# A recommendation tower on one core: the last layer with its input as the stationary operand and the weight as one moving column

## What is computed

```python
e = jnp.stack([tbl_f[ids[:, f]] for f in range(27)], axis=1)     # 2048 x 27 x 128
dot = jnp.einsum('bnd,bmd->bnm', e, e)                           # all pairs of features
z = flat[:, idx]                                                 # the 351 pairs i < j
h = jnp.concatenate([z, dense_ctx], axis=1)                      # 2048 x 367
h = jnp.maximum(h @ W_top1 + b_top1, 0.0)                        # 512
h = jnp.maximum(h @ W_top2 + b_top2, 0.0)                        # 256
y = h @ W_top3                                                   # 2048 x 1
```

## Time and profile before

| | |
|---|---|
| median of 3 runs | 385.35 us (384.9 to 387.28) |
| the profiled execution's time | 387.6 us |
| its span, first to last instruction | 385.8 us |
| TensorE busy | 345.6 us, 90% of the span |
| GpSimd busy | 251.8 us, 65% |
| VectorE busy | 251.6 us, 65% |
| ScalarE busy | 124.3 us, 32% |
| granted TensorE clock, mean | 0.969 of full speed |

### The profile page before, as it was taken

How to read it: one execution, slowest core, us unless ns; L and a number is a source line. 1 busy time by engine, 2 the same in 40 slices (tenths; PEclk the granted TensorE clock), 3 DMA queues, 4 the chain that set the end, 5 groups by cost and what they waited for, 6 DMA issues and landing times.

```text
span 385.8 us, 14180 instructions
## 1 busy us (share of the span) xinstructions
PE 345.6 (90%) x6216; PEld 308.1 (80%) x6216; DVE 251.6 (65%) x757; ACT 124.3 (32%) x235; POOL 251.8 (65%) x271
## 2 busy tenths in 40 slices
PE   0875899889799999999999999999999999997686
PEld 0764788778699888998899878997899978995675
DVE  4898597767576677666876658675876668742031
ACT  2554234232133332333233223333233322335122
POOL 5777777777777777777777777775777667730000
PEclk9999699899699999999999999999999999999699
DMA  7998843357634763446534754547433744344420
GB/s 187 262 259 206 209 103 93 77 138 157 101 82 93 166 137 87 95 110 169 114 83 98 166 126 99 88 99 175 110 78 91 162 115 100 63 85 99 76 49 1
DMA packets 59215, 46.39 MB, mean 120 GB/s; under 512 B 38499, under 2 KB 53186, under 8 KB 59153
## 3 DMA queue, kind: packets, MB, share of 16 engines
q1 hardware_dynamic: 50705, 28.16, 32.8%
q0 software_dynamic: 8448, 17.32, 19.8%
HBM read 38.37 MB, written 7.09 MB: 118 GB/s over the span
## 4 chain that ended last, share of the span: by engine, by line
PE 68%; POOL 18%; issue 8%; DVE 3%; DMA 2%; ACT 1%; POOLq 0%
PE onehot_ps L592 20%; POOL rows L352 18%; PE onehot_ps L594 14%; PE dots_ps L620 10%; PE tile_ps L604 6%; PE mlp_ps L626 5%; PE mlp_ps L628 5%; PE mlp_ps L627 5%; PE mlp_ps L661 2%; DVE mask L493 2%; DMA rows<-tbl,idx 2%; DMA idx<-ids_gather 1%; DVE z_lo L531 1%; DVE h_lo L538 0%; ACT h_hi L401 0%
## 5 line engine op out<-in xcount | busy, mean ns | idle before, releaser
L352 POOL DMA_INDIRECT rows<-tbl,idx x264 | 251.0, 951 | 89.7 <-issue 76.6
L493 DVE TENSOR_SCALAR mask<-idb,cmp 125x256 fp32r<-125x256 int32 x672 | 210.4, 382 | 78.2 <-PE onehot_ps L594 72.9
L592 PE MATMUL onehot_ps<-mask,tab_hi 125*128 125x256 f32 x672 | 187.0, 312 | 19.5 <-DVE tab_lo L500 9.5
L594 PE MATMUL onehot_ps<-mask,tab_lo 125*128 125x256 f32 x672 | 171.3, 285 | 0.0
L592 PEld LDWEIGHTS onehot_ps<-mask,tab_hi 125*128 125x128 f32 x672 | 130.1, 194 | 34.7 <-DVE mask L493 17.3
L594 PEld LDWEIGHTS onehot_ps<-mask,tab_lo 125*128 125x128 f32 x672 | 130.7, 194 | 0.0
L376 ACT COPY emb<-tile_ps 128x512 f32<-128x512 f32 x66 | 38.8, 589 | 62.9 <-PE tile_ps L604 62.8
L620 PEld LDWEIGHTS dots_ps<-emb 128*27 128x27 f32 x4096 | 44.1, 106 | 18.6 <-issue 17.0
L620 PE MATMUL dots_ps<-emb 128*27 128x27 f32 x4096 | 52.8, 194 | 6.1 <-issue 5.7
L367 ACT COPY emb<-onehot_ps 128x512 f32<-128x512 f32 (+1 forms) x46 | 30.8, 670 | 67.7 <-PE onehot_ps L594 64.0
L604 PE MATMUL tile_ps<-ident,rows 128*128 128x128 f32 x264 | 41.7, 282 | 10.2 <-DMA rows<-tbl,idx 10.2
(11 more groups left out here) (30 smaller groups left out, 145.3 us busy)
## 6 DMA issues: line engine op xcount, KB each, us to landing
idb<-ids_onehot SPq DMA_DIRECT2D x84, 128.0 KB
dots_dram<-dots SPq DMA_DIRECT2D x28, 216.0 KB
emb<-tbl SPq DMA_DIRECT2D x11, 448.0 KB
rows<-tbl,idx POOLq DMA_INDIRECT x264
zT<-dots_dram SPq DMA_DIRECT2D x14, 117.0 KB
dots_dram<-dots SPq DMA_DIRECT2D x8, 108.0 KB, 2.9
zT<-dots_dram SPq DMA_DIRECT2D x7, 104.0 KB
emb<-tbl SPq DMA_DIRECT2D x11, 52.0 KB
```

Source lines behind the costliest of these rows:

```text
L352: nc.gpsimd.indirect_dma_start(rows[:, n % RING, i, :], None, tables[feature][:, :], bass.IndirectOffsetOnAxis(idx[:, at:at + 1], 0)).then ...
L493: made = nc.vector.tensor_scalar(mask[0:VP, n % MASK_RING, c, :], idb[0:VP, k % IDB_RING, :], cmp[0:VP, at:at + 1], None, ALU.is_equal)
L592: nc.tensor.matmul(out, tab_hi[0:VP, f, at, :], mask[0:VP, k % MASK_RING, c, :], start=(at == 0), stop=False)
L594: done = nc.tensor.matmul(out, tab_lo[0:VP, f, at, :], mask[0:VP, k % MASK_RING, c, :], start=False, stop=(at == CHUNKS - 1))
```

## The change

Layer 3 exchanges its operands. For each of the two tiles and each of the two halves of `h2`, the 128 x 128 piece of `h2` is the stationary operand and the weight's column the moving one. So a block has four matmuls with one column each where it had two with 256, and the result lies on 128 partitions, one column for each tile. ScalarE copies 128 x 2 values to a tensor of its own, `y_sb` (128 x 8 x 2), which has a place for every block. So the wait for earlier stores ahead of the second ReLU is gone, and the one between the last two stores. Each block is stored with two transfers of 128 values, one for each tile, and the order of the samples is put right by the pattern of the destination: each value of 4 bytes is a piece of its own.

```diff
-        y_sb = h2[0:1, 0, :]
+        y_sb = sb("y_sb", [P, BLOCKS, TILES], f32)
...
             def store_y(b):
                 sp.wait_ge(mlp_ps_empty, MLP_FREED * (b + 1))
-                sp.dma_start(y[0:1, b * BLK:(b + 1) * BLK], y_sb).then_inc(y_out, 16)
+                for q in range(TILES):
+                    if b < LAST:
+                        at, into = b * BLK + QUAD // TILES * q, [[1, QUAD // TILES], [QUAD, NQ], [1, 1]]
+                    else:
+                        at, into = b * BLK + P * q, [[1, QUAD], [QUAD, NQ // TILES], [1, 1]]
+                    sp.dma_start(bass.AP(y.tensor, at, into), y_sb[:, b, q:q + 1],
+                                 allow_slow_non_contiguous=True).then_inc(y_out, 16)
...
             store_y(LAST - 1)
-            sp.wait_ge(y_out, 16 * LAST)
             store_y(LAST)
-            sp.wait_ge(y_out, 16 * BLOCKS)
+            sp.wait_ge(y_out, 16 * TILES * BLOCKS)
...
             def relu2(b):
-                if b > 0:
-                    act.wait_ge(y_out, 16 * b)
...
             def empty_y(b):
                 act.wait_ge(mlp_ps_full, MLP_STEPS * (b + 1))
-                if b < LAST:
-                    dst = y_sb.rearrange("p (g s) -> p g s", s=QUAD)
-                    src = mlp_ps[0:1, 0, 0:BLK].rearrange("p (s g) -> p g s", s=QUAD)
-                else:
-                    dst = y_sb.rearrange("p (q g s) -> p q g s", q=TILES, s=QUAD)
-                    src = mlp_ps[0:1, 0, 0:BLK].rearrange("p (q s g) -> p q g s", q=TILES, s=QUAD)
-                nc.scalar.copy(dst, src).then_inc(mlp_ps_empty, 1)
+                nc.scalar.copy(y_sb[:, b, :], mlp_ps[:, 0, 0:TILES]).then_inc(mlp_ps_empty, 1)
...
             def layer3(b):
-                for c in range(M2):
-                    pe.wait_ge(mlp_ps_empty, MLP_FREED * b + c + 1)
-                    done = nc.tensor.matmul(mlp_ps[0:1, 0, 0:BLK], w3_sb[:, c:c + 1], h2[:, c, :],
-                                            start=(c == 0), stop=(c == M2 - 1))
+                for q in range(TILES):
+                    for c in range(M2):
+                        pe.wait_ge(mlp_ps_empty, MLP_FREED * b + c + 1)
+                        done = nc.tensor.matmul(mlp_ps[:, 0, q:q + 1], h2[:, c, q * P:(q + 1) * P],
+                                                w3_sb[:, c:c + 1], start=(c == 0), stop=(c == M2 - 1))
                 done.then_inc(mlp_ps_full, 1)
```

## The result

The changed kernel takes 419.74 us (median of 4 runs, 417.16 to 423.06) against 385.45: a ratio of 1.089, 95% interval 1.080 to 1.097. The forecast was 386.0 us and no measurable change. It is slower by 34 us. The experiments' ratios are against the kernel before, run beside each (medians 384.94, 385.23 and 386.21 us), and leave out executions over 1.5% above the fastest of their kernel, such as one of 420.93 us of the in-order stores and one of 416.94 us of the run with only the stores.

The account below looks back on a forecast made before the run. TensorE was taken to bound the loop over blocks, and a serial tail the last 36 us. With -0.4 us in the loop and +1.1 in the tail, +0.7 on 385.35 gave 386.0 us, range 383.4 to 388.8.

Parts of the forecast that it names:

- Then the packets: Tail, last two stores: 20 ns a packet, 32 packets per engine for the second store, 0.8 us in all.
- The bound for one engine: Tail, landing of the last two stores: 256 packets of 20 ns all on one engine, +4.9 us.
- I count nothing: SyncE's queue: seven more store pairs, each some 0.6 us longer to issue, covered by waits; slower gathers also given no cost.
- rival (4): Instruction supply: eight added records per block shift TensorE's stops in block 7, up to 2.5 us: 383.5 or 388.5; chance 0.10.
- TensorE in the loop: Layer 3 in blocks 0 to 5: loads spaced 0.11 us, 0.88 us against 0.95, six times: -0.4 us.
- Rivals (1) and (3): Layer 3's loads: without overlap, 390.9 us, chance 0.10; or at the transposes' pace, 383.4 us, chance 0.10.
- The copy: Tail, ScalarE's result copy: 128 rows of 2 in 159 ns where one row of 256 took 361 ns, -0.2 us.
- Waits that go: Second ReLU's wait for stores worth nothing; SyncE's wait between the last two stores 0.43 to 0.03 us, -0.4 us.
- TensorE in the tail: Layer 3 behind the last ReLU: six loads and a matmul's latency stay, ending at 383.58, +0.24 us.
- Issuing: Last two stores on SyncE: 0.43 us each with 0.05 between them; bounds 0.24 and 0.78 us.
- Rival (2): One engine carries the stores' packets: +4.9 us, 389.9 us in all; chance 0.07.

Follow-up runs that it names:

- in-order stores: Changed kernel with the second ReLU writing in output order, so each store's 128 values go to neighbouring places: 413.64 us, ratio 1.074.
- the run with only the stores: Kernel before, own layer 3 and store kept, plus the changed kernel's two stores beside each store, to a scratch tensor: 409.38 and 416.94 us.
- 127-value run: Kernel before with two packed stores of 127 single values added beside each store: 447.27 us, ratio 1.159.
- wide pitch: Kernel before with two stores of 128 single values added beside each store, values 256 bytes apart in DRAM: 386.33 us, ratio 1.005.
- the seven runs with added stores: Kernel before with two stores added beside each store, differing in pitch, piece size or count of values: from 386.25 to 447.27 us.

## Why the prediction was wrong

**The step that failed** is "Then the packets", with what hangs on it. It took the price of a 4-byte packet from the records of other packets, 12.8 to 32 ns busy, and spread 32 of them over the landing: 0.8 us. That the engines differ in number was seen; that the price hangs on how close together the writes lie was not among the bounds, and no row of before had such stores: the smallest were pieces of 128 bytes. The landing behind the last issue was put at 1.39 + 0.8 = 2.2 us and took 8.3 us (421.2 - 412.94). The bound for one engine, 1.39 + 5.1 = 6.5 us, was too small as well: the 127-value run took 14.2 us.

**The second failed step** is "I count nothing" under SyncE's queue. It asked who is queued behind the stores on SyncE, and there the answer holds: the issues took 1.25 us for two (0.91 expected) and at the wide pitch 16 more issues cost 0.4 to 3.5 us. It did not ask who shares the DMA engines while they are held, and this step is the larger miss: 26.9 us of the 35.4. The changed kernel between 194.2 and 199.5 us, eight microseconds behind the start of a store (packets, MB, share of the 16 engines' time):

```profile
DMA packets 88, 0.09 MB, mean 18 GB/s; under 512 B 5, under 2 KB 85, under 8 KB 88
```

```profile
q1 hardware_dynamic: 83, 0.08, 55.5%
q0 software_dynamic: 5, 0.01, 0.6%
```

In the kernel before, as long behind the same block's store (182.64 us), between 190.5 and 195.8:

```profile
q0 software_dynamic: 131, 0.29, 22.8%
q1 hardware_dynamic: 229, 0.21, 21.0%
```

83 packets fill 55.5% of 16 x 5.3 us: 567 ns each, where 229 packets of about the same size, 1 KB, took 78 ns each; GpSimd's gathers get 5 packets through where they got 131. VectorE stops there:

```profile
200.58 0.62 DVE L492 TENSOR_SCALAR mask<-idb,cmp 125x256 fp32r<-125x256 int32 x2 [6.51 <-remote]
```

and ScalarE with it, for 7.5 us, both without a releaser. The products that ScalarE waits for had ended at about 193.1, and the kernel has it wait there for nothing else. In block 7, behind the store at 373.82, it is TensorE:

```profile
387.37 1.05 PE L619 MATMUL dots_ps<-emb 128*27 128x27 f32 x70 [7.82 <-issue]
```

That is the place where it stopped for 2.60 us before, for want of instructions as the prediction read it, and rival (4) had it as the point where a late instruction packet tells. One instruction packet is in the window of that stop, 379.6 to 387.3 us, in the same view as above:

```profile
q1 hardware_dynamic: 1257, 0.16, 52.1%
q8 instruction: 1, 0.02, 1.6%
```

The instruction packet took 2.0 us (1.6% x 16 x 7.7), where the 49 of the kernel before took 1.0 in the mean. So the reading that fits is that the engines' instruction streams come through the same DMA engines and were late; it is argued from the place and the missing releaser. For the stop of VectorE and ScalarE the records give it no support: no instruction packet is among those between 190 and 202 us. How a held DMA engine stops an engine that waits for no transfer stays open. What is shown is that the stops come and go with the pitch of the stores.

**The rest of the steps.** *TensorE in the loop*: -0.07 us a block was forecast, -0.16 came; the load was 192 ns for 194 expected, the spacing nearer 0.10 than 0.11. Rivals (1) and (3) fall with it. *The copy*: 160 ns for 159. *Waits that go*: the copy ended at 411.73, the store was issued at 411.76, 0.03 behind it as expected. But the price was read wrong: the seven runs with added stores keep both waits, and their last row goes out 0.09 to 0.10 us behind its copy (381.59 and 381.69 in the run with the 256-byte pitch). So the wait was worth 0.07 us; what made 0.43 of it in the trace before is not known. *TensorE in the tail*: 0.84 us from the ReLU's release to the end, 0.83 expected. *Issuing*: 1.18 us for the last two, 0.91 expected; in the in-order run 0.81. *Rival (2)*, one engine for the stores, was the nearest to the mechanism in kind, and gave 4.5 us where 34 came.

*The half-speed clock* adds some: with TensorE stopped from 194.9 to 201.3 us the granted clock falls to the lower level, 1.2 GHz, behind the stop. In the window from 201 to 207 us it is 0.50, and a product takes 0.41 us and not 0.28:

```profile
201.00:207.00 6.00, 5.75 (x25) 5.38 (x25) 4.10 (x15) 0.65 (x1) 0.00 (x0) 0.50 0.74 155
```

In the tail it makes 1.4 of the 1.9 us that the stretch up to the last copy is longer. Layer 1 of block 7, from 401.5 on:

```profile
401.50:405.00 3.50, 3.50 (x19) 3.50 (x19) 0.69 (x1) 0.60 (x1) 0.00 (x0) 0.51 0.02 0
```

The clock is at the lower level there, with TensorE busy 5.8 of the 7.5 us ahead of it at 1.00. 15 products follow each other at 0.21 us, where before they did at 0.12, at a granted 1.00 from 374 to 378. Why it fell in one kernel and not in the other no run shows. The prediction had no term for any of this, since it had no stops.

## What to carry to other kernels

A store that leaves the values of a column on 128 partitions as 4-byte pieces packed in DRAM is not a small store: 256 of them took about 7 us to land and held up other transfers on the DMA engines, and compute engines stopped behind them. Price a transfer by how its writes lie in memory too, and not by bytes, packets or issue time alone, and ask who shares the engines, not only who is queued behind it. Where results lie on the partitions, gather them on chip and transpose before the store, which could not be told from the kernel before, or pad their places in DRAM: added to that kernel, padded stores cost under 1%.

## What the runs showed of the hardware

- 256 single values of 4 bytes, packed in DRAM: 6.7 us from the last issue to landing with 128 in a store; 254 of them, 127 in a store, 14.2 us; 1.1 us where they lie 64 or 256 bytes apart, or are packed pieces of 32 or 64 bytes. In the whole kernel: 413.1, 447.3, and 386 to 388 us against 385 to 386 without them.
- The packets' records don't show it: they end 6 us and more before the landing.
- A float32 load of 128 columns takes 192 ns, and four matmuls of one column each with such loads, eight records, pass in 0.79 us: the loads overlap each other, and what counts is their spacing of about 0.1 us.
- SyncE issues a store of one piece in 0.24 us, one of 128 pieces in 0.4 us, and one with the pattern 2 x 64 in 0.6 us.
